# First attention: the row maxima from four 32-row tiles of TensorE, a head in each, and spread over the whole group

## The chip, the cores and the metric

The kernel runs on one core of one Trainium2 chip. The metric is the device time of one execution, in microseconds, read on that core. Three executions of the kernel before took 1702.1, 1706.09 and 1711.71 us; their median, 1706.09 us, is the time before.

## The reference

A two-layer transformer block on x of shape (4, 512, 256), with a context of the same shape and one mask row: an attention with 16 heads of 16, a mixture of 8 experts with top-1 routing, an attention with 16 heads of 64 and 128 memory rows, and three pairs of dequantized linear layers with LoRA. The change touches the first attention alone:

```python
qh = (q @ Wq.T + bq).reshape(Bq, Sq, H, Dh).transpose(0, 2, 1, 3)      # q = layernorm(x), H = 16, Dh = 16
kh = (k @ Wk.T + bk).reshape(Bq, Sk, H, Dh).transpose(0, 2, 1, 3)
attn = jnp.einsum('bhqd,bhkd->bhqk', qh, kh) * Dh ** -0.5
attn = jnp.where(causal_mask, -jnp.inf, attn)
attn = jax.nn.softmax(attn, axis=-1)
out = jnp.einsum('bhqk,bhkd->bhqd', attn, vh)
x = x + out.transpose(0, 2, 1, 3).reshape(Bq, Sq, D) @ Wo.T + bo
```

## The kernel before, in words

`attention0` goes through the batches (4) in a loop and in each through four groups of four heads. Everything is in one launch, with engines that meet at semaphores.

Queries and keys are projected half by half (8 heads) into `full`, and split into a high part `hi` (float32r) and a rest `lo` (L418). SyncE's DMAs then stack them by head into `q_stack` and `k_stack`, 128 partitions by head by 512: rows 0 to 15 hold hi and hi, rows 16 to 31 hi and lo, rows 48 to 63 lo and hi, the last row the negative row maximum of the queries against ones. One matmul over 128 rows (L602) so gives a head's scores less the row maximum for one key tile; a second (L604) adds the key mask. Six DMAs of 128 KB stack four heads' queries and keys (`stack`, L233, and `stack_last`, L241).

The softmax needs the row maximum first. For each head and each of the four query tiles one matmul (L579) over rows 0 to 126 writes 128 x 512 scores into one of the three banks of `p_m`, and VectorE adds the query mask and takes the maximum into `mx` (L424). After 16 of these, for the four heads of the group ahead, `mx` is transposed (L586), negated (L432) and brought into the last row of `q_stack` by a DMA (L248).

The order on TensorE is written out by hand in the table STEPS: eight parts per group, each with two score tiles of two heads. ScalarE takes the exponentials of a part (L334), TensorE multiplies them with the values in four column tiles of 32, one a head (`times_v`, L615), and for each group the row sums are spread (`sums`, L591), VectorE takes their reciprocal (L440) and multiplies (L442). `query` and `key` are the projections for the half ahead (in groups 0 and 2), `rows` the four transposes of the next batch's normalized x (in group 1), `turn` is L586. `maximum`, `turn`, `sums`, `rows`, `query` and `key` share the three banks in turn: an instruction that fills a bank waits until the reader of the fill three places before is done. VectorE's program goes through the same table.

After group 3 of a batch come its last `times_v` and `sums`, the values of the next batch (L569), and the output projection (L659), which waits for the last L442.

The functions that the diff touches, with the line numbers of the profile:

Of the kernel before, what the change touches and what calls it, by code (L numbers as in the profile page):

```python
# [5 lines left out]
F32 = mybir.dt.float32  # L6
# [9 lines left out]
P = 128  # L16
# [57 lines left out]
def attention0(nc, x_all, A, held):  # L74
# [9 lines left out]
    with ExitStack() as ctx:  # L84
# [6 lines left out]
        def sem(name):  # L91
# [43 lines left out]

        STEPS = (("query", "score", "score", "times_v", "maximum"),
                 ("key", "maximum", "score", "maximum", "score", "maximum"),
                 ("maximum", "score", "maximum", "score", "times_v", "maximum"),  # L140
                 ("maximum", "score", "maximum", "score", "maximum"),
                 ("maximum", "score", "maximum", "score", "times_v", "maximum"),
                 ("maximum", "score", "maximum", "score", "maximum"),
                 ("score", "score", "turn", "times_v"),
                 ("sums", "score", "score", "rows"))
        PARTS = len(STEPS)
        N_MAX = G0 * NT

        def steps(g, j, ahead):

            for what in STEPS[j]:
                if what in ("query", "key") and (g % 2 or g and not ahead):
                    continue

                if what == "rows" and (g != 1 or not ahead):
                    continue
                if what == "sums" and g == 0:
                    continue
                if what in ("maximum", "turn") and g + 1 >= NG0 and not ahead:
                    continue  # L160
                yield what

        FILLS = {"query": 1, "key": 1, "maximum": 1, "turn": 1, "rows": NT, "sums": 1}
        DVE_FILLS = {"maximum": 1, "rows": NT, "sums": 1}

        def fills(kinds, last_g=NG0 - 1):

            return sum(kinds.get(w, 0) for g in range(last_g + 1) for j in range(PARTS) for w in steps(g, j, True))


        BEFORE = NT + 2 + 2 + N_MAX + 1
        DVE_BEFORE = NT + 2 + N_MAX

        AT_END = 2 + 1 + NT // 2
        assert (fills(FILLS) + AT_END) % M_BANKS == 0
        x_in, weights_in, loaded = sem("x_in"), sem("weights_in"), sem("loaded")
        consts, prep = sem("consts"), sem("prep")
        zeroed, prefilled = sem("zeroed"), sem("prefilled")
# [6 lines left out]
        m_free = Count(sem("m_free"), fills(DVE_FILLS) + AT_END, DVE_BEFORE)  # L185
        hi_ready = Count(sem("hi_ready"), 4)
        split_ready = Count(sem("split_ready"), 4)
        stacked = [Count(sem("stacked_first"), 16 * 12), Count(sem("stacked_last"), 16 * 12)]
        mx_ready = Count(sem("mx_ready"), NG0)
        nm_ready = Count(sem("nm_ready"), NG0)  # L190
        nm_in = Count(sem("nm_in"), 16 * NG0)
# [17 lines left out]
        @block.sync  # L209
        def _(sp):  # L210
            def load_x(i):
                sp.dma_start(x_all[:, i * NT:(i + 1) * NT, :],
                             A["x"][i].rearrange("(t p) d -> p t d", p=P)).then_inc(x_in, 16)

            load_x(0)
            for dst, src in ((bqk[:], A["L0_bqk"]), (wq[:], A["L0_wq"]), (wk[:], A["L0_wk"])):
                sp.dma_start(dst, src).then_inc(weights_in, 16)
            sp.dma_start(ctx_t[:], A["ctx_t"][0]).then_inc(ctx_in.sem, 16)
            for dst, src in ((wv[:], A["L0_wv"]), (bv[:], A["L0_bv"].partition_broadcast(P)), (mask_in[:], A["mask"]),
                             (bo[:], A["L0_bo"].partition_broadcast(P)), (wo[:], A["L0_wo"])):  # L220
                sp.dma_start(dst, src).then_inc(loaded, 16)
            for i in range(1, B):
                load_x(i)

            halves = ((q_stack, (hi, hi, lo)), (k_stack, (hi, lo, hi)))

            def stack(b, half):

                at = 8 * (half % 2)
                for n, (stack, parts) in enumerate(halves):  # L230
                    split_ready.wait(sp, b, 2 * half + n + 1)
                    for k, part in enumerate(parts):
                        sp.dma_start(stack[DH0 * k:DH0 * (k + 1), at:at + G0, :].bitcast(F32),  # L233
                                     part[0:P // 2, n, :].bitcast(F32)).then_inc(stacked[0].sem, 16)

            def stack_last(half):

                at = 8 * (half % 2) + G0
                for n, (stack, parts) in enumerate(halves):
                    for k, part in enumerate(parts):  # L240
                        sp.dma_start(stack[DH0 * k:DH0 * (k + 1), at:at + G0, :].bitcast(F32),  # L241
                                     part[P // 2:P, n, :].bitcast(F32)).then_inc(stacked[1].sem, 16)

            def bring_maxima(b, g):

                nm_ready.wait(sp, b, g + 1)
                at = G0 * (g % NG0)
                sp.dma_start(q_stack[MAX_ROW:P, at:at + G0, :].bitcast(F32), neg_max[:].bitcast(F32))\  # L248
                  .then_inc(nm_in.sem, 16)

            def turn(b, ahead):
                for g in range(NG0):
                    if g % 2 == 0 and (ahead or g == 0):
                        stack(b, g // 2 + 1)
# [55 lines left out]
        def _(act):  # L310
# [6 lines left out]
            def project(b, half, n, m):  # L317


                split_ready.wait(act, b, 2 * half + n - 1)  # L320
                for count in stacked:
                    count.wait(act, b, 16 * 6 * half)
# [49 lines left out]
        def _(dve):  # L372
# [38 lines left out]
            def split(b, half, n):  # L411

                hi_ready.wait(dve, b, 2 * half + n + 1)

                if n == 0:
                    for count in stacked:
                        count.wait(dve, b, 16 * 6 * half)
                dve.tensor_tensor(lo[:, n, :], full[:, n, :], hi[:, n, :].bitcast(F32),  # L418
                                  ALU.subtract).then_inc(split_ready.sem, 1)

            def maximum(b, fill, i):
                m = fill.bank()
                m_full.wait_apart(dve, b, fill.n, prep, 5)
                dve.tensor_tensor_reduce(scratch[:, fill.n % M_BANKS, :], m, bias_q[:, i % NT, :], 1.0, -3.0e38, ALU.add,  # L424
                                         ALU.max, mx[:, i:i + 1]).then_inc(m_free.sem, 1)

            def turn_maxima(b, fill, g):
                m = fill.bank()
# [15 lines left out]
            def turn(b, ahead):  # L444
                fill = Fill()
                freed = 0
                for g in range(NG0):
                    i = 0
                    for j in range(PARTS):
                        for what in steps(g, j, ahead):  # L450
                            freed += DVE_FILLS.get(what, 0)
                            if what == "maximum":
                                maximum(b, fill, i)
                                i += 1
                            elif what == "turn":
                                turn_maxima(b, fill, g + 1)
                            elif what == "rows":
# [52 lines left out]
            for i in range(N_MAX):  # L510
                maximum(-1, fill, i)
            turn_maxima(-1, fill, NG0)
            dve.wait_ge(x_in, 16 * B)
            with dve.Fori(0, B - 1) as b:
                turn(b, True)
# [3 lines left out]
        def _(pe):  # L519
# [52 lines left out]

            def maximum(b, banks, g, i):

                h, t = G0 * (g % NG0) + i // NT, i % NT
                m = banks.free()
                if i == 0:
                    stacked[g % 2].wait(pe, b, 16 * 6 * (g // 2 + 1))
                done(pe.matmul(m, q_stack[0:MAX_ROW, h, P * t:P * (t + 1)], k_stack[0:MAX_ROW, h, :],  # L579
                               start=True, stop=True))  # L580

            def turn_maxima(b, banks, g):
                m = banks.free(nm_ready, g + 1)
# [35 lines left out]
            def turn(b, ahead):  # L619
# [2 lines left out]
                banks = Banks(b)  # L622
                banks.readers = [(m_free, -1), (m_free, 0), (m_free, 0)]
                for g in range(NG0):
                    i = 0
                    for j in range(PARTS):
                        head = 0
                        for what in steps(g, j, ahead):
                            if what in ("query", "key"):
                                project(b, banks, g // 2 + 1, ("query", "key").index(what))  # L630
                            elif what == "maximum":
                                maximum(b, banks, g + 1, i)
                                i += 1
                            elif what == "turn":
                                turn_maxima(b, banks, g + 1)
                            elif what == "score":
# [36 lines left out]
            for i in range(N_MAX):  # L673
                maximum(-1, banks, NG0, i)
            turn_maxima(-1, banks, NG0)
            with pe.Fori(0, B - 1) as b:
                turn(b, True)
            turn(B - 1, False)
# [1376 lines left out]
```

## Time and profile before

| | |
|---|---|
| time, three executions | 1702.1, 1706.09, 1711.71 us |
| the profiled execution's own time | 1709.27 us |
| its span, first to last instruction | 1707.6 us |
| mean granted TensorE clock | 0.929 |
| TensorE matmuls busy | 1480.1 us, 87% |
| TensorE weight loads busy | 881.2 us, 52% |
| VectorE busy | 904.5 us, 53% |
| ScalarE busy | 494.4 us, 29% |
| GpSimd busy | 451.0 us, 26% |
| first attention | about 0 to 437 us of the span |

The shares of the page are means over all stages, and the first attention is a quarter of the span. A matmul's record includes the time until its result has landed, so records of matmuls overlap: the pace at which TensorE works is read from the distance between starts. The idle time in brackets in a timeline is counted from the end of the record before, and so is shorter than the real hold-up. In a timeline neighbouring instructions of one line stand as one row with their count.

### The profile page before, as it was taken

Reading aid. Unit: us, or ns where it says so; the run is one execution under the profiler, and the core shown is the slowest. Engines: PE = TensorE matmul, PEld = TensorE weight load, DVE = VectorE, ACT = ScalarE, POOL = GpSimd, SP = SyncE. Lnnn points to the kernel's source line nnn. Section 1 sums busy time; section 2 is a strip of 40 time slices with the busy share of each in tenths; the row PEclk is TensorE's granted clock in tenths of the full one; section 3 lists DMA queues with packets and bytes.
Section 4 is the critical chain, followed back from the end, with each engine's and each line's share of the span. In section 5 each row is a group of like instructions: output and inputs, shape, how many; then the busy total and the mean of one; then the engine's idle time right before and its main releaser. Section 6 shows DMA issues by size and latency. Waiting matters only on the chain. (4 is left out here: it accounts for less than half of the span.)

```text
span 1707.6 us, 18955 instructions
## 1 busy us (share of the span) xinstructions
PE 1480.1 (87%) x6061; PEld 881.2 (52%) x6088; DVE 904.5 (53%) x1684; ACT 494.4 (29%) x618; POOL 451.0 (26%) x257
## 2 busy tenths in 40 slices
PE   5899898998719889874799999999999999976886
PEld 2334343443618777752444446444644465435775
DVE  5666666765420000015467664766576656736666
ACT  2443334444102222210133332333233323320221
POOL 2000000000240000022144442544344534552333
PEclk8999999999559999995799999999999999986998
DMA  6522113220374545335456555565356655302001
GB/s 157 140 38 37 32 19 50 37 38 1 130 247 144 180 155 182 135 64 90 81 74 87 74 79 69 76 86 69 43 74 86 82 67 68 44 0 102 1 0 50
DMA packets 62238, 136.14 MB, mean 80 GB/s; under 512 B 10593, under 2 KB 21217, under 8 KB 57569
## 3 DMA queue, kind: packets, MB, share of 16 engines
q1 hardware_dynamic: 59440, 127.26, 39.5%
q0 software_dynamic: 2736, 8.13, 1.4%
q8 instruction: 31, 0.51, 0.1%
q14 instruction: 31, 0.25, 0.1%
HBM read 58.55 MB, written 12.06 MB: 41 GB/s over the span
## 5 line engine op out<-in xcount | busy, mean ns | idle before, releaser
L1070 POOL TENSOR_TENSOR a_probs<-a_probs 128x1024 f32<-128x1024 f32 x128 | 304.2, 2376 | 415.6 <-PE a_p_os L1633 415.1
L1141 ACT ACTIVATE a_probs<-a_p_s 128x1024 f32<-128x1024 f32 x160 | 163.7, 1023 | 378.9 <-PE a_p_s L1619 378.9
L1352 DVE TENSOR_REDUCE a_max_ctx<-a_p_m 128x1 f32<-128x512 f32 x256 | 169.9, 688 | 79.8 <-PE a_p_m L1594 76.7
L424 DVE CUSTOM_DVE_ANT_0 a_scratch<-a_p_m,a_bias_q 128x512 bf16<-128x512 f32 x256 | 163.1, 687 | 80.6 <-PE a_p_m L579 80.5
L334 ACT ACTIVATE a_probs<-a_p_s 128x1024 f32<-128x1024 f32 x128 | 130.5, 1024 | 140.8 <-PE a_p_s L604 135.9
L579 PE MATMUL a_p_m<-a_k_stack,a_q_stack 127*128 127x512 f32 x256 | 128.0, 543 | 14.5 <-DVE a_mx L424 7.0
L1633 PE MATMUL a_p_os<-a_probs,a_v 128*64 128x512 f32 x512 | 138.1, 618 | 0.0
L1514 PE MATMUL a_p_s<-a_o_raw,a_w 128*128 128x256 f32 x480 | 123.8, 392 | 13.8 <-DVE a_o_raw L1283 13.8
L1594 PE MATMUL a_p_m<-a_k_hl,a_q_hh 128*128 128x512 f32 x256 | 111.0, 481 | 18.6 <-DVE a_v L1330 8.2
L1288 DVE TENSOR_TENSOR a_yb<-a_p_os,a_yb 128x512 f32<-128x512 f32 x15 | 10.4, 692 | 218.9 <-PE a_p_os L1523 218.9
L1523 PE MATMUL a_p_os<-a_w,a_probs 128*128 128x256 f32 x480 | 118.6, 380 | 0.6 <-ACT a_probs L1118 0.6
L1618 PE MATMUL a_p_s<-a_q_hh,a_k_hl 128*128 128x512 f32 x256 | 118.5, 463 | 0.0
L602 PE MATMUL a_p_s<-a_q_stack,a_k_stack 128*128 128x512 f32 x256 | 117.4, 487 | 1.0 <-DMA a_q_stack<-a_neg_max 0.9
L1375 DVE RECIPROCAL a_recip<-a_p_os 128x512 f32<-128x512 f32 x32 | 106.8, 3336 | 16.6 <-PE a_p_os L1643 16.6
L1514 PEld LDWEIGHTS a_p_s<-a_o_raw,a_w 128*128 128x128 f32 x480 | 92.6, 195 | 30.2 <-DVE a_o_raw L1283 17.6
L1594 PEld LDWEIGHTS a_p_m<-a_k_hl,a_q_hh 128*128 128x128 f32 x256 | 46.6, 195 | 109.0 <-DVE a_max_ctx L1352 53.1
L1619 PE MATMUL a_p_s<-a_q_lm,a_k_h 65*128 65x512 f32 x256 | 102.2, 399 | 0.0
L1118 ACT ACTIVATE a_probs<-a_p_s,a_b 128x256 f32<-128x256 f32 x120 | 55.9, 473 | 151.0 <-PE a_p_s L1514 150.9
L1523 PEld LDWEIGHTS a_p_os<-a_w,a_probs 128*128 128x128 f32 x480 | 91.2, 190 | 14.1 <-ACT a_probs L1118 1.8
L604 PE MATMUL a_p_s<-a_bias_k,a_ident_b 128*128 128x512 bf16 x229 | 90.0, 393 | 0.0
L579 PEld LDWEIGHTS a_p_m<-a_k_stack,a_q_stack 127*128 127x128 f32 x256 | 47.2, 198 | 66.5 <-DVE a_mx L424 45.7
L1343 DVE SCALAR_TENSOR_TENSOR a_lo<-a_p_m,a_bqk,a_hi 128x512 fp32r<-128x512 f32 x58 | 43.0, 747 | 59.0 <-ACT a_hi L1131 54.2
(200 smaller groups left out, 2162.0 us busy)
## 6 DMA issues: line engine op xcount, KB each, us to landing
a_w<-in_L_w SPq DMA_DIRECT2D x30, 1024.0 KB, 8.0
a_q_hh<-a_hi SPq DMA_DIRECT2D x64, 256.0 KB, 5.6
a_k_hl<-a_hi SPq DMA_DIRECT2D x32, 256.0 KB, 8.0
a_k_hl<-a_lo SPq DMA_DIRECT2D x32, 256.0 KB, 9.5
a_k_h<-a_hi SPq DMA_DIRECT2D x32, 256.0 KB, 10.6
a_q_lm<-a_lo SPq DMA_DIRECT2D x32, 256.0 KB, 7.1
a_ctx_t<-in_ctx_t SPq DMA_DIRECT2D x8, 512.0 KB, 5.7
a_q_stack<-a_hi SPq DMA_DIRECT2D x32, 128.0 KB, 3.9
```

The source lines that it names most:

```text
L334: act.activation(probs[:, j % 4, :, :], p_s[:, j % 2, :, :], ACT.Exp).then_inc(exp_done.sem, 1)
L424: dve.tensor_tensor_reduce(scratch[:, fill.n % M_BANKS, :], m, bias_q[:, i % NT, :], 1.0, -3.0e38, ALU.add, ALU.max, mx[:, i:i + 1]).then_ ...
L579: done(pe.matmul(m, q_stack[0:MAX_ROW, h, P * t:P * (t + 1)], k_stack[0:MAX_ROW, h, :], start=True, stop=True))
L602: pe.matmul(p_s[:, slot, i, :], k_stack[:, h, P * kt:P * (kt + 1)], q_stack[:, h, :], start=True, stop=False)
L1070: pool.tensor_tensor(probs[:, kt], probs[:, kt - 1], probs[:, kt], ALU.add)\
L1141: act.activation(probs[:, kt, :, :], p_s[:, (KT1 * p + kt) % 2, :, :], ACT.Exp).then_inc(exp_done.sem, 1)
L1352: dve.tensor_reduce(max_ctx[:, NT * head + t:NT * head + t + 1], m, AX, ALU.max)\
L1514: mm = pe.matmul(p_h[:, c % 4, 0:CT], w1[:, r, k, P * c:P * (c + 1)], rows_t[:, r % 2, k, :], start=(k == 0), stop=(k == DC - 1))
L1523: mm = pe.matmul(p_y[:, t, 0:D], hidden[:, d % 4, P * t:P * (t + 1)], w2[:, r, d, :], start=(d == 0), stop=(d == FC - 1))
L1594: done(pe.matmul(m, q_hh[:, s, P * t:P * (t + 1)], k_hl[:, s, :], start=True, stop=True))
L1618: pe.matmul(p_s[:, n % 2, i, :], first, q_hh[:, s, :], start=True, stop=False)
L1633: mm = pe.matmul(p_o[DK * i:DK * (i + 1), :], vh, probs[:, kt, i, :], start=(kt == 0), stop=(kt == KT1 - 1))
```

## The change: what it does

The maxima are taken from the high parts alone. The high parts of a group's four heads now lie in four different 32-row strips of the stacks (rows 0 to 15, 32 to 47, 64 to 79, 96 to 111), so that a maximum's matmul reads 16 rows of its head's strip and runs in a 32-row tile of the array; successive maxima go through the four heads. For this the DMAs that stack a half's queries and keys are cut differently: four of 32 KB and two of 128 KB in place of three of 128 KB. The table spreads the maxima in runs of three and two after the scores; the first two of a group's sixteen (`early`) are taken in the last part of the group before, where `sums` now stands behind the scores and behind these two.

```diff
-        STEPS = (("query", "score", "score", "times_v", "maximum"),
-                 ("key", "maximum", "score", "maximum", "score", "maximum"),
...
-                 ("sums", "score", "score", "rows"))
+        STEPS = (("query", "score", "score", "times_v", "maximum", "maximum", "maximum"),
+                 ("key", "score", "score", "maximum", "maximum", "maximum"),
...
+                 ("score", "score", "early", "early", "sums", "rows"))
+        EARLY = sum(step.count("early") for step in STEPS)
...
-            halves = ((q_stack, (hi, hi, lo)), (k_stack, (hi, lo, hi)))
+            def fill(n, at, rows, landed):
+
+                stack, parts = ((q_stack, (hi, lo)), (k_stack, (lo, hi)))[n]
+                for i in range(G0):
+                    sp.dma_start(stack[32 * i:32 * i + DH0, at + i, :].bitcast(F32),
+                                 hi[rows + i:rows + P // 2:G0, n, :].bitcast(F32)).then_inc(landed, 16)
+                for k, part in zip((1, 3), parts):
+                    sp.dma_start(stack[DH0 * k:DH0 * (k + 1), at:at + G0, :].bitcast(F32),
+                                 part[rows:rows + P // 2, n, :].bitcast(F32)).then_inc(landed, 16)
...
             def maximum(b, banks, g, i):
 
-                h, t = G0 * (g % NG0) + i // NT, i % NT
+                tile, t = i % G0, i // G0
+                h, rows = G0 * (g % NG0) + tile, slice(32 * tile, 32 * tile + DH0)
                 m = banks.free()
                 if i == 0:
-                    stacked[g % 2].wait(pe, b, 16 * 6 * (g // 2 + 1))
-                done(pe.matmul(m, q_stack[0:MAX_ROW, h, P * t:P * (t + 1)], k_stack[0:MAX_ROW, h, :],
-                               start=True, stop=True))
+                    stacked[g % 2].wait(pe, b, LANDED * (g // 2 + 1))
+                done(pe.matmul(m, q_stack[rows, h, P * t:P * (t + 1)], k_stack[rows, h, :], start=True, stop=True))
```

TensorE where group 2 of a batch ends and group 3 begins, before. L591 spreads the sums of the group before, L602 and L604 are the scores and their mask, L615 is `times_v`, L579 a maximum:

```order
L591 MATMUL a_p_m<-a_o_norm,a_spread 128x512
L602 MATMUL a_p_s<-a_q_stack,a_k_stack 128x512
L604 MATMUL a_p_s<-a_bias_k,a_ident_b 128x512
...
L615 MATMUL a_p_o<-a_probs,a_v 32x512 x4
L63 REGISTER_ALU
L579 MATMUL a_p_m<-a_k_stack,a_q_stack 128x512 x2
L602 MATMUL a_p_s<-a_q_stack,a_k_stack 128x512
L604 MATMUL a_p_s<-a_bias_k,a_ident_b 128x512
L63 REGISTER_ALU
L579 MATMUL a_p_m<-a_k_stack,a_q_stack 128x512
```

The same place with the change; L603 is now the sums, L614 and L616 the scores, L627 `times_v`, L592 a maximum:

```order
L614 MATMUL a_p_s<-a_q_stack,a_k_stack 128x512
L616 MATMUL a_p_s<-a_bias_k,a_ident_b 128x512
L63 REGISTER_ALU x2
L592 MATMUL a_p_m<-a_k_stack,a_q_stack 128x512 x2
L603 MATMUL a_p_m<-a_o_norm,a_spread 128x512
L63 REGISTER_ALU x2
L614 MATMUL a_p_s<-a_q_stack,a_k_stack 128x512
...
L627 MATMUL a_p_o<-a_probs,a_v 32x512 x4
L63 REGISTER_ALU
L592 MATMUL a_p_m<-a_k_stack,a_q_stack 128x512
...
L592 MATMUL a_p_m<-a_k_stack,a_q_stack 128x512
L63 REGISTER_ALU
L592 MATMUL a_p_m<-a_k_stack,a_q_stack 128x512
```

Two maxima now stand ahead of the sums, and the sums stand behind the part's scores instead of ahead of them. Between the sums and the third maximum after them lie one part's scores and `times_v`, where there were two parts' scores, `times_v` and more.

SyncE's queue for one half of a batch, before (the first four heads, the maxima of the group ahead, the last four heads):

```order
L233 DMA a_q_stack<-a_hi 16x4x512 x2
L233 DMA a_q_stack<-a_lo 16x4x512
L63 REGISTER_ALU
L233 DMA a_k_stack<-a_hi 16x4x512
L233 DMA a_k_stack<-a_lo 16x4x512
L233 DMA a_k_stack<-a_hi 16x4x512
L63 REGISTER_ALU
L248 DMA a_q_stack<-a_neg_max 1x16x128
```

And with the change:

```order
L233 DMA a_q_stack<-a_hi 16x512 x4
L236 DMA a_q_stack<-a_hi 16x4x512
L236 DMA a_q_stack<-a_lo 16x4x512
L63 REGISTER_ALU
L233 DMA a_k_stack<-a_hi 16x512 x4
L236 DMA a_k_stack<-a_lo 16x4x512
L236 DMA a_k_stack<-a_hi 16x4x512
L63 REGISTER_ALU
L254 DMA a_q_stack<-a_neg_max 1x16x128
```

Twelve DMAs are issued for four heads instead of six.

## Rows read from the trace of the kernel before

**Rows 1.** Busy time by stretch: PE, PEld, DVE, ACT, POOL, then granted clock
```profile
44.00:437.00 393.00, 354.57 (x1531) 164.40 (x1557) 253.07 (x612) 156.82 (x172) 10.18 (x6) 0.96 0.23 42
```

**Rows 2.** Groups by line, 44 to 437 us: busy, mean ns, idle before
```profile
L579 PE MATMUL a_p_m<-a_k_stack,a_q_stack 127*128 127x512 f32 x240 | 118.3, 527 | 8.1 <-DVE a_mx L424 7.0
```

**Rows 3.** TensorE's timeline around one `times_v`: start, length, instructions
```profile
50.68 0.39 PE L602 MATMUL a_p_s<-a_q_stack,a_k_stack 128*128 128x512 f32 x1
50.91 0.39 PE L604 MATMUL a_p_s<-a_bias_k,a_ident_b 128*128 128x512 bf16 x1
51.23 1.07 PE L615 MATMUL a_p_o<-a_probs,a_v 128*32 128x512 f32 x8
52.23 0.72 PE L579 MATMUL a_p_m<-a_k_stack,a_q_stack 127*128 127x512 f32 x2
52.79 0.39 PE L602 MATMUL a_p_s<-a_q_stack,a_k_stack 128*128 128x512 f32 x1
```

**Rows 4.** The same timeline: a key projection, four passes of 512 columns
```profile
94.04 1.88 PE L560 MATMUL a_p_m<-a_ctx_t,a_wk 128*128 128x512 f32 x4
```

**Rows 5.** A matmul in a 32-row tile, and what follows it
```profile
L1915 PE MATMUL f_p_y<-f_lora_b,f_lora_a x24: 629/629/791, 1550.6 to 1568.0; 32*128 32x256 f32 x24
1568.58 1.57 PEld L1934 LDWEIGHTS f_p_t<-f_ident,f_h 128*128 128x128 f32 x8 [0.65 <-issue]
```

**Rows 6.** Timeline, start of group 3: TensorE, then VectorE
```profile
109.88 1.13 PE L591 MATMUL a_p_m<-a_o_norm,a_spread 128*128 128x512 f32 x2
...
113.05 1.06 PE L615 MATMUL a_p_o<-a_probs,a_v 128*32 128x512 f32 x8 [0.19 <-ACT a_probs L334]
114.04 0.74 PE L579 MATMUL a_p_m<-a_k_stack,a_q_stack 127*128 127x512 f32 x2
...
111.04 3.36 DVE L440 RECIPROCAL a_recip<-a_p_m 128x512 f32<-128x512 f32 x1 [1.68 <-PE a_p_m L591]
114.44 0.69 DVE L442 TENSOR_TENSOR a_o_norm<-a_o_norm,a_recip 128x512 f32<-128x512 f32 x1
115.05 0.68 DVE L424 CUSTOM_DVE_ANT_0 a_scratch<-a_p_m,a_bias_q 128x512 bf16<-128x512 f32 x1
...
115.66 0.68 DVE L424 CUSTOM_DVE_ANT_0 a_scratch<-a_p_m,a_bias_q 128x512 bf16<-128x512 f32 x1
```

**Rows 7.** Timeline of TensorE, end of group 1: sums, third row transpose
```profile
80.40 1.13 PE L591 MATMUL a_p_m<-a_o_norm,a_spread 128*128 128x512 f32 x2
...
84.98 0.44 PE L546 MATMUL a_p_m<-a_ident,a_xn 128*128 128x128 f32 x2 [2.08 <-DVE a_recip L440]
```

**Rows 8.** Timeline, end of a batch
```profile
128.03 1.13 PE L591 MATMUL a_p_m<-a_o_norm,a_spread 128*128 128x512 f32 x2
...
131.19 1.06 PE L615 MATMUL a_p_o<-a_probs,a_v 128*32 128x512 f32 x8 [1.11 <-ACT a_probs L334]
...
138.43 0.89 PE L659 MATMUL a_p_m<-a_wo,a_o_norm 128*128 128x256 f32 x3 [0.81 <-DVE a_o_norm L442]
...
134.20 3.36 DVE L440 RECIPROCAL a_recip<-a_p_m 128x512 f32<-128x512 f32 x1 [0.92 <-PE a_p_m L591]
```

**Rows 9.** Timeline of TensorE: the transpose of the maxima
```profile
126.82 0.28 PE L586 MATMUL a_p_m<-a_ident,a_mx 128*16 128x128 f32 x1 [0.19 <-DVE a_mx L424]
```

**Rows 10.** DMA issues in group 2, and their median time to landing
```profile
99.41 1.18 SPq L233 DMA_DIRECT2D a_q_stack<-a_hi  x2
...
103.45 0.60 SPq L233 DMA_DIRECT2D a_k_stack<-a_hi  x1
...
a_k_stack<-a_hi SPq DMA_DIRECT2D x2, 128.0 KB, 4.3
```

**Rows 11.** Timeline of TensorE: the longest wait of a maximum for a bank
```profile
73.37 0.50 PE L579 MATMUL a_p_m<-a_k_stack,a_q_stack 127*128 127x512 f32 x1 [1.18 <-DVE a_mx L424]
```

**Rows 12.** Before the loop: a stacking DMA and the first maximum
```profile
23.50 0.60 SPq L233 DMA_DIRECT2D a_k_stack<-a_hi  x1
...
29.49 9.83 PE L579 MATMUL a_p_m<-a_k_stack,a_q_stack 127*128 127x512 f32 x16 [6.34 <-DMA a_k_stack<-a_hi]
```

More of the change, by code:

```diff
@@ L132, in attention0 @@
         p_o = ps("p_o", [P, S])
-        STEPS = (("query", "score", "score", "times_v", "maximum"),
-                 ("key", "maximum", "score", "maximum", "score", "maximum"),
[L140 to L143, printed above, removed]
+        STEPS = (("query", "score", "score", "times_v", "maximum", "maximum", "maximum"),
+                 ("key", "score", "score", "maximum", "maximum", "maximum"),
+                 ("score", "score", "maximum", "maximum", "times_v"),
+                 ("score", "score", "maximum", "maximum"),
+                 ("score", "score", "maximum", "maximum", "times_v"),
+                 ("score", "score", "maximum", "maximum"),
                  ("score", "score", "turn", "times_v"),
-                 ("sums", "score", "score", "rows"))
+                 ("score", "score", "early", "early", "sums", "rows"))
+        EARLY = sum(step.count("early") for step in STEPS)
         PARTS = len(STEPS)
@@ L160, in steps @@
                     continue
+                if what == "early" and g + 2 >= NG0 and not ahead:
+                    continue
                 yield what
-        FILLS = {"query": 1, "key": 1, "maximum": 1, "turn": 1, "rows": NT, "sums": 1}
-        DVE_FILLS = {"maximum": 1, "rows": NT, "sums": 1}
+        FILLS = {"query": 1, "key": 1, "maximum": 1, "early": 1, "turn": 1, "rows": NT, "sums": 1}
+        DVE_FILLS = {"maximum": 1, "early": 1, "rows": NT, "sums": 1}
         def fills(kinds, last_g=NG0 - 1):
             return sum(kinds.get(w, 0) for g in range(last_g + 1) for j in range(PARTS) for w in steps(g, j, True))
-        BEFORE = NT + 2 + 2 + N_MAX + 1
-        DVE_BEFORE = NT + 2 + N_MAX
+        BEFORE = NT + 2 + 2 + N_MAX + 1 + EARLY
+        DVE_BEFORE = NT + 2 + N_MAX + EARLY
         AT_END = 2 + 1 + NT // 2
         assert (fills(FILLS) + AT_END) % M_BANKS == 0
+        LANDED = 16 * 2 * (G0 + 2)
         x_in, weights_in, loaded = sem("x_in"), sem("weights_in"), sem("loaded")
@@ L187, in attention0 @@
         split_ready = Count(sem("split_ready"), 4)
-        stacked = [Count(sem("stacked_first"), 16 * 12), Count(sem("stacked_last"), 16 * 12)]
+        stacked = [Count(sem("stacked_first"), 2 * LANDED), Count(sem("stacked_last"), 2 * LANDED)]
         mx_ready = Count(sem("mx_ready"), NG0)
@@ L223, in _ @@
                 load_x(i)
-            halves = ((q_stack, (hi, hi, lo)), (k_stack, (hi, lo, hi)))
+            def fill(n, at, rows, landed):
[6 more added lines that the diff above has]
+                                 part[rows:rows + P // 2, n, :].bitcast(F32)).then_inc(landed, 16)
             def stack(b, half):
-                at = 8 * (half % 2)
-                for n, (stack, parts) in enumerate(halves):
+                for n in range(2):
                     split_ready.wait(sp, b, 2 * half + n + 1)
-                    for k, part in enumerate(parts):
-                        sp.dma_start(stack[DH0 * k:DH0 * (k + 1), at:at + G0, :].bitcast(F32),
-                                     part[0:P // 2, n, :].bitcast(F32)).then_inc(stacked[0].sem, 16)
+                    fill(n, 8 * (half % 2), 0, stacked[0].sem)
             def stack_last(half):
[L238 to L242, printed above, removed]
+                for n in range(2):
+                    fill(n, 8 * (half % 2) + G0, P // 2, stacked[1].sem)
             def bring_maxima(b, g):
@@ L321, in project @@
                 for count in stacked:
-                    count.wait(act, b, 16 * 6 * half)
+                    count.wait(act, b, LANDED * half)
                 at = half % 2
@@ L416, in split @@
                     for count in stacked:
-                        count.wait(dve, b, 16 * 6 * half)
+                        count.wait(dve, b, LANDED * half)
                 dve.tensor_tensor(lo[:, n, :], full[:, n, :], hi[:, n, :].bitcast(F32),
@@ L423, in maximum @@
                 m_full.wait_apart(dve, b, fill.n, prep, 5)
-                dve.tensor_tensor_reduce(scratch[:, fill.n % M_BANKS, :], m, bias_q[:, i % NT, :], 1.0, -3.0e38, ALU.add,
-                                         ALU.max, mx[:, i:i + 1]).then_inc(m_free.sem, 1)
+                h, t = i % G0, i // G0
+                dve.tensor_tensor_reduce(scratch[:, fill.n % M_BANKS, :], m, bias_q[:, t, :], 1.0, -3.0e38, ALU.add,
+                                         ALU.max, mx[:, NT * h + t:NT * h + t + 1]).then_inc(m_free.sem, 1)
             def turn_maxima(b, fill, g):
@@ L447, in turn @@
                 for g in range(NG0):
-                    i = 0
+                    i, early = EARLY, 0
                     for j in range(PARTS):
@@ L454, in turn @@
                                 i += 1
+                            elif what == "early":
+                                maximum(b, fill, early)
+                                early += 1
                             elif what == "turn":
@@ L512, in _ @@
             turn_maxima(-1, fill, NG0)
+            for i in range(EARLY):
+                maximum(-1, fill, i)
             dve.wait_ge(x_in, 16 * B)
@@ L624, in turn @@
                 for g in range(NG0):
-                    i = 0
+                    i, early = EARLY, 0
                     for j in range(PARTS):
@@ L633, in turn @@
                                 i += 1
+                            elif what == "early":
+                                maximum(b, banks, g + 2, early)
+                                early += 1
                             elif what == "turn":
@@ L675, in _ @@
             turn_maxima(-1, banks, NG0)
+            for i in range(EARLY):
+                maximum(-1, banks, NG0 + 1, i)
             with pe.Fori(0, B - 1) as b:
```

## The prediction

> **What bounds the kernel now.** I read the busy time by stretch first. In the first attention, the only place that changes, TensorE is busy 355 of 393 us at a granted clock of 0.96, VectorE 253, ScalarE 157 [rows 1]. So TensorE's program sets the time, and everything behind the attention starts when it ends. The groups by line then say what a maximum is there: 240 matmuls in the loop, that is 15 groups of 16, with little idle time of TensorE directly before them [rows 2]. The record of one is 527 ns, but that is latency. The pace is in the timeline: L602 and L604 start 0.23 us apart [rows 3]. Sixteen maxima cost 3.7 us of a group of some 18 us.
>
> **The burst in a 32-row tile, and its price.** The change lets two or three maxima of different heads stream at once: in the best case a run of two or three costs one stream, 0.21 us, in place of 0.46 or 0.69. The same trace shows what another tile shape between full-array matmuls costs, with the column tiles of `times_v`. L604 starts at 50.91 and needs 0.23; the next full-array matmul starts at 52.23, 1.09 us later; the two streams in it are 2 x 0.43 = 0.86, as (1.88 - 0.16) / 4 = 0.43 for one pass of 512 columns [rows 4], 0.16 being a record's tail (0.39 - 0.23). Behind it two maxima take 0.56 instead of 0.46 [rows 3]. So two changes of tile shape cost 0.23 + 0.10 = 0.33 us: the queue that otherwise loads weights under the running matmul stands until the array is empty, and the first load is then uncovered. Row tiles are seen once: the last matmul of L1915 starts at 1568.0 and streams some 0.43 us, at the lower clock level; the next load, in full shape, comes at 1568.58, 0.15 us after, and the weight queue's idle time of 0.65 is put to no other engine [rows 5]. A gap there as well.
>
> A run between full-array matmuls thus costs 0.21 + 0.33, and 0.10 more since its own weights have 128 columns where those of `times_v` have 32: 0.64. Against 0.46 for two that is +0.18, against 0.69 for three -0.05. A run beside a `times_v` adds one change of shape only, some 0.44: -0.02 for two, -0.25 for three. A group has three lone pairs, one lone triple, two pairs and one triple beside `times_v`: 3 x 0.18 - 0.05 - 0.04 - 0.25 = +0.2 us. For 15 groups **+3.0 us**: the overlap is eaten by the changes of shape.
>
> The Trainium skill (TensorEngine Tiling (Array Packing), Key Properties) says that a change of tiling mode drains TensorE while tiles of one mode run independently. No run here shows it for a pair of row tiles; the column tiles agree, with 0.33 us for two changes. It makes a free change of shape, the fast rival below, the less likely.
>
> **The sums behind the scores.** Three banks go round, and the third maximum after the sums waits for VectorE's reciprocal.
> - Group 3, which has no projection to fill the time. From the start of the sums the reciprocal ends 4.56 us later (109.88 to 114.44) [rows 6]. TensorE has then done sums 0.86, two score tiles 4 x 0.23 = 0.93, `times_v` 0.95 with its change of shape and another 0.2: it is at the first maximum after 3.0 and at the third at once, and waits 1.55. VectorE starts on them at 5.17 (115.05) and needs 0.61 each (115.05 to 115.66) [rows 6], as before, so of the later holding up I add 0.2. The wait of `times_v` for ScalarE, 0.25 with the start of L604 and the bracket of 0.19 [rows 6], goes, as the two early maxima and the sums now lie between. 1.5 us in each of three batches (the last has no maxima there): **+4.4**.
> - Group 1, with the row transposes. The third transpose starts 4.58 us after the sums do (80.40 to 84.98), held 2.08 us by the reciprocal's bank [rows 7]. The scores that were under this wait now stand ahead of the sums: 0.93 each in three batches, **+2.8**.
> - The end of a batch. Scores, early pair, sums and `times_v` now follow each other, where `times_v` waited (bracket 1.11) [rows 8]. But VectorE gets the sums late: its first reciprocal starts 0.93 + 0.5 + 1.16 = 2.6 us into the part, is done with the product at 2.6 + 4.0 = 6.6 to 6.8, and the second, which starts at 134.20 - 128.03 = 6.17 now [rows 8], moves by 0.6, and L659 with it. The early pair, counted at 0.64 above, is inside that. **0**.
>
> **The transpose of the maxima.** It waits for the last maximum (bracket 0.19, about 0.35 by the starts) [rows 9]. The last pair arrives together, so VectorE needs 2 x 0.61 after it, while TensorE has two score tiles: 0.1 more for each of 15 groups, **+1.5**.
>
> **Stacking.** SyncE needs about 0.6 to 0.64 us for each issue (1.18 for two) [rows 10]. In groups 0 and 2 the first `early` needs the stack of that same half. Before, the first issue is at 99.41, the last at 103.45, landed 4.3 later, ahead of the group's end at 109.88. Now VectorE reaches the split two maxima later (1.2 us), and the last issue stands 11 x 0.64 = 7.0 behind the first: 99.41 + 1.2 + 7.0 + 4.3 = 111.9. TensorE is there at 109.88 + 0.93 + 0.3 = 111.1. With the semaphore's way I take 0.9, seven times: **+6.3**. The ends are 0 (DMAs of 32 KB that land sooner) and 2.4 each, if landing takes the 6.0 us of the start, 23.50 to 29.49 [rows 12].
>
> **Before the loop.** The first maximum waits for the stack [rows 12]. Six more issues stand ahead, 3.8 us; landing takes 4.3 instead of 6.0 if the engines are less behind, so between +2.1 and +3.8. I take 2.8, and 0.5 for the two early maxima there: **+3.3**.
>
> **Waits for a bank inside a group.** With three maxima a part VectorE needs 1.83 us where a part without `times_v` gives 1.6; the longest wait is 1.5 us (bracket 1.18) [rows 11]. With two it needs 1.22 and these waits go, but the first two parts now hold three each in one run, which only VectorE's pace of 0.61 serves. I set these against each other: **0**, ends -7 and +3 over all.
>
> The sum is 3.0 + 4.4 + 2.8 + 1.5 + 6.3 + 3.3 = **+21 us**: 1709.3 (span 1707.6 and 1.7 around it) + 21 = 1731 for the profiled execution, which lies 3.2 over the median; from the median 1706.1 it is 1728.
>
> **Rivals.**
> - *Changes of shape are free for row tiles (the other side).* Then a run costs 0.21 and no more, 11 changes of shape a group go from the sum, 11 x 0.165 x 15 = 27 us, of which I leave 3 to the banks, as TensorE then comes sooner to the same reciprocal. 1728 - 24 = 1704, no slower than before; with the stacks in time 1698. It decides from a price below about 0.05 us a change. For it: the array's rows are separate tiles with weights of their own. Against: 0.33 at every `times_v` [rows 3], and the gap at 1568.58 [rows 5].
> - *Row tiles don't overlap.* Nine more streams a group, 9 x 0.21 x 15 = 28 us, of which a third lies in waits for VectorE: +19, 1747. Against: the column tiles do overlap, eight matmuls in 1.07 us [rows 3].
> - *The stack lands late*, at its upper end, 7 x 1.5 = +10: 1738.
> - *Nothing runs in a row tile*: 16 x 0.23 a group as before, less 3 us of the sum, 1725; little apart from the forecast, and in its chance.
>
> The Trainium skill (TensorE: Matmul & The Clock Gate, Part 3) reports four row tiles of K = 32 at 3.07 times the speed of one after another. By that a run of two or three costs hardly more than one stream, which is the value in the sum; no run here shows it.
>
> **How the numbers follow.** Forecast 0.50 (1728, its own range 1716 to 1738), free changes 0.24 (1698 to 1707), no overlap 0.14, late stack 0.12. The range 1703 to 1748 leaves out the fastest of the free cases and the worst of the slow ones. A change of 0.5% is 8.5 us, about what can be told from none: faster 0.11 and same 0.15, nearly all from the second case and the low edge of the forecast; slower 0.74.
>
> **What would show it.** Right: in the new timeline the matmul after a run of two starts about 0.85 us after the L604-like one before the run; the third maximum of group 3 stands 1.5 us for the reciprocal; `early` in groups 0 and 2 waits for a DMA; the batch takes some 6 us more than now; times behind the attention are unchanged. Wrong: weight loads of a run start under the scores before it, runs of 0.2 us, and a group shorter than now.

## The result, and the profile after

The changed kernel takes 1767.3 us (median of 4, 1764.5 to 1769.9) against 1708.9 us for the kernel before on the same chip: a ratio of 1.0347, 95% interval 1.0309 to 1.0386. It is slower by 3.5%. The forecast was slower by 21 us, range 1703 to 1748. The sign is right, the size is not, and the time lies outside the range. One of the twelve executions of e5 below took 4924 us and is left out of its numbers.

Behind the attention nothing moved. The stretch from the end of the last output projection (L659) to the end of the span, in the kernel before:

```profile
439.00:1708.00 1269.00, 1100.38 (x4472) 703.14 (x4472) 627.96 (x1011) 326.78 (x440) 429.06 (x236) 0.92 0.46 89
```

and of the changed kernel, with its attention (answering to [rows 1]) and two of its groups. The columns are length, busy time of PE, PEld, DVE, ACT and POOL, granted clock, DMA share, GB/s:

```profile
44.00:499.00 455.00, 400.28 (x1538) 164.12 (x1565) 254.10 (x612) 155.78 (x172) 10.20 (x6) 0.88 0.13 37
499.00:1769.00 1270.00, 1099.27 (x4472) 701.57 (x4472) 628.47 (x1011) 326.75 (x440) 428.85 (x236) 0.92 0.46 89
302.00:321.00 19.00, 17.34 (x80) 6.22 (x81) 13.61 (x45) 8.41 (x10) 3.39 (x2) 1.00 0.34 81
351.00:378.00 27.00, 24.09 (x83) 8.27 (x83) 14.71 (x36) 8.77 (x10) 0.00 (x0) 0.75 0.16 39
```

All of it is in the attention, which from 44 us on takes 455 us where it took 395 (44 to 439), and the granted clock there is 0.88 where it was 0.96. A group is counted here from one transpose of the maxima to the next. One that keeps the clock (302 to 321) takes 19.2 us, where the same group of before took 18.5; one that loses it (351 to 378) takes 26.8, where it took 18.1. The granted clock is a mix of the two levels 2.4 and 1.2 GHz. (1 - clock) x length is the most that the lower level can have cost, as if TensorE had never waited there: 55 us now, 16 before.

The timeline of TensorE shows the mechanics at full clock, first a lone pair and the transpose, answering to [rows 3, 9], then the start of a group 3, to [rows 6]:

```profile
318.82 0.39 PE L616 MATMUL a_p_s<-a_bias_k,a_ident_b 128*128 128x512 bf16 x1
319.14 0.50 PE L592 MATMUL a_p_m<-a_k_stack,a_q_stack 16*128 16x512 f32 x2
319.58 0.50 PE L614 MATMUL a_p_s<-a_q_stack,a_k_stack 128*128 128x512 f32 x1
319.92 0.39 PE L616 MATMUL a_p_s<-a_bias_k,a_ident_b 128*128 128x512 bf16 x1
...
321.15 0.28 PE L598 MATMUL a_p_m<-a_ident,a_mx 128*16 128x128 f32 x1 [0.38 <-DVE a_mx L431]
...
354.46 0.50 PE L592 MATMUL a_p_m<-a_k_stack,a_q_stack 16*128 16x512 f32 x2 [0.59 <-DMA a_k_stack<-a_hi]
354.88 1.12 PE L603 MATMUL a_p_m<-a_o_norm,a_spread 128*128 128x512 f32 x2
...
359.74 0.50 PE L592 MATMUL a_p_m<-a_k_stack,a_q_stack 16*128 16x512 f32 x1 [1.37 <-DVE a_recip L447]
...
361.29 1.80 PE L592 MATMUL a_p_m<-a_k_stack,a_q_stack 16*128 16x512 f32 x3
363.02 0.80 PE L614 MATMUL a_p_s<-a_q_stack,a_k_stack 128*128 128x512 f32 x1
363.61 0.65 PE L616 MATMUL a_p_s<-a_bias_k,a_ident_b 128*128 128x512 bf16 x1
```

The pair's record is 0.50 us for two, where a lone one takes 0.50 too (359.74): they stream together. From L616 to the score behind the pair it is 0.76, of which 0.23 are L616 itself, and the next distance is 0.34 instead of 0.23: 0.64 us for the pair. The early pair waits for a stacking DMA. The third maximum behind the sums waits for the reciprocal and starts 4.86 us after them. Then comes something that no term had: after three maxima at VectorE's pace (361.29) the same L616 takes a record of 0.65 instead of 0.39. The array runs at half clock from here.

The same course in the first batch, windows of the changed kernel (the early pair there waits 0.89 for its DMA):

```profile
68.92 0.50 PE L592 MATMUL a_p_m<-a_k_stack,a_q_stack 16*128 16x512 f32 x2 [0.89 <-DMA a_k_stack<-a_hi]
...
70.00:74.00 4.00, 3.44 (x19) 1.11 (x17) 3.83 (x16) 2.40 (x3) 1.02 (x1) 1.00 0.44 103
74.00:81.00 7.00, 6.77 (x19) 2.17 (x19) 5.07 (x18) 1.20 (x2) 0.00 (x0) 0.55 0.46 117
```

### The profile page after: what moved, and what is told of

Read it like the earlier page. It is cut to its first block and busy times, and to the rows that moved or that the text cites. A ratio compares the mean times of both kernels' runs of the same rounds, so it can differ in the third digit from the quotient of the medians.

```text
span 1768.3 us, 19048 instructions
## 1 busy us (share of the span) xinstructions
PE 1521.2 (86%) x6061; PEld 877.0 (50%) x6088; DVE 905.8 (51%) x1684; ACT 493.4 (28%) x618; POOL 450.9 (25%) x257
## 5 line engine op out<-in xcount | busy, mean ns | idle before, releaser
L614 PE MATMUL a_p_s<-a_q_stack,a_k_stack 128*128 128x512 f32 x256 | 143.6, 621 | 0.0
L592 PE MATMUL a_p_m<-a_k_stack,a_q_stack 16*128 16x512 f32 x256 | 82.6, 563 | 23.4 <-DMA a_k_stack<-a_hi 12.0
L616 PE MATMUL a_p_s<-a_bias_k,a_ident_b 128*128 128x512 bf16 x229 | 96.8, 423 | 0.0
L614 PEld LDWEIGHTS a_p_s<-a_q_stack,a_k_stack 128*128 128x128 f32 x256 | 55.0, 215 | 71.3 <-issue 36.7
L627 PE MATMUL a_p_o<-a_probs,a_v 128*32 128x512 f32 x512 | 77.4, 680 | 0.8 <-ACT a_probs L340 0.8
```

The costliest lines, as they stand in the source:

```text
L614: pe.matmul(p_s[:, slot, i, :], k_stack[:, h, P * kt:P * (kt + 1)], q_stack[:, h, :], start=True, stop=False)
```

## The experiments

Times are medians; the ratio is to the kernel before, run beside it, which stood at 1708.1 to 1710.2. "Clock" is the granted clock in the profile from 44 us to the end of the attention's last output projection, "lost" is (1 - clock) x length there, an upper bound, known to about 2 us by the rounding. "Whole" is the granted clock of a whole execution, the median of all of them; 0.001 of it is 1.7 us.

| kernel | us | ratio, 95% interval | clock | lost, us | whole |
|---|---|---|---|---|---|
| before | 1709 | | 0.96 | 16 | 0.929 |
| changed | 1767.3 | 1.0347 (1.0309 to 1.0386) | 0.88 | 55 | 0.910 |
| e1 order only | 1720.5 | 1.0072 (1.0052 to 1.0091) | 0.96 | 16 | 0.928 |
| e2 full tiles | 1728.5 | 1.0109 (1.0090 to 1.0129) | 0.96 | 17 | 0.929 |
| e3 32 rows | 1759.5 | 1.0297 (1.0278 to 1.0315) | 0.91 | 40 | 0.915 |
| e4 sums first | 1739.5 | 1.0184 (1.0159 to 1.0208) | 0.94 | 25 | 0.922 |
| e5 order, sums first | 1713.0 | 1.0021 (1.0009 to 1.0032) | 0.96 | 16 | 0.929 |
| e6 same tile | 1770.4 | 1.0350 (1.0327 to 1.0373) | 0.89 | 50 | 0.912 |
| e7 rows, old order | 1749.2 | 1.0231 (1.0214 to 1.0247) | 0.94 | 26 | 0.924 |
| e8 filler | 1766.9 | 1.0325 (1.0306 to 1.0343) | 0.93 | 32 | 0.920 |
| e9 even table | 1698.5 | 0.9941 (0.9922 to 0.9960) | 0.98 | 8 | 0.933 |
| e10 66 rows | 1739.3 | 1.0167 (1.0140 to 1.0193) | 0.92 | 34 | 0.924 |
| e11 64 rows | 1753.8 | 1.0244 (1.0212 to 1.0275) | 0.93 | 31 | 0.923 |
| e12 DMAs only | 1710.1 | 1.0005 (0.9990 to 1.0019) | 0.96 | 16 | 0.929 |

An interval reaches 2 to 5 us to either side (7 for the changed kernel), so a difference of a few us between two rows of the table is rough.

The theory after the result: the clock falls because matmuls over 16 rows do not keep it up (A). The rival: it falls because TensorE stands in more and longer waits, whatever its matmuls are (B).

**e1, the order without the row tiles.** The stacks are those of before, three DMAs of 128 KB for queries and three for keys:

```diff
-                stack, parts = ((q_stack, (hi, lo)), (k_stack, (lo, hi)))[n]
...
+                stack, parts = ((q_stack, (hi, hi, lo)), (k_stack, (hi, lo, hi)))[n]
...
-                done(pe.matmul(m, q_stack[rows, h, P * t:P * (t + 1)], k_stack[rows, h, :], start=True, stop=True))
+                done(pe.matmul(m, q_stack[0:MAX_ROW, h, P * t:P * (t + 1)], k_stack[0:MAX_ROW, h, :], start=True, stop=True))
```

> The new order with the two early maxima, but the maxima as before: full-array matmuls over 127 rows of the old stacks, six DMAs of 128 KB for four heads. Theory A (the clock falls because matmuls of 16 rows in row tiles do not keep it up): the granted clock in the first attention is back at about 0.95 or more, and what is left over the kernel before are the waits of the order, by the prediction's terms 4 to 10 us: 1713 to 1719. Theory B (the clock falls because TensorE now stands in more and longer waits, whatever the tile): clock near 0.88 there and 1735 or more. The DMA wait of the first early maximum is gone or under 0.3 us, since six issues end 3.8 us sooner.

Measured 1720.5, clock 0.96. The clock is back, as A expected, and the order by itself costs 12 us, a little over A's 1713 to 1719.

**e2, full-array maxima in the changed kernel.** Only the last two lines of e1's diff.

> The changed kernel with one edit: each maximum is a full-array matmul over 127 rows of the new stacks; order, DMAs and waits are those of the changed kernel. Theory A: clock in the first attention at 0.94 or more; the time is that of the new order alone and of the later stacks, 1718 to 1728, 40 to 50 us under the changed kernel. Theory B: the clock stays near 0.88, and the time is 1755 or more, as only the changes of tile shape go and the overlap with them.

Measured 1728.5, at the upper end of what A expected, 39 us under the changed kernel. The long waits are still there. The timeline of e2 in the first batch has them, the early pair's even longer than the 0.89 of the changed kernel:

```profile
66.42 0.72 PE L592 MATMUL a_p_m<-a_k_stack,a_q_stack 127*128 127x512 f32 x2 [1.37 <-DMA a_k_stack<-a_hi]
...
71.17 1.72 PE L592 MATMUL a_p_m<-a_k_stack,a_q_stack 127*128 127x512 f32 x3 [0.28 <-DVE a_mx L431]
72.73 0.39 PE L614 MATMUL a_p_s<-a_q_stack,a_k_stack 128*128 128x512 f32 x1
```

and the windows of e2 over the stretches shown of the changed kernel keep the full clock (the same work stands about 3 us earlier in e2):

```profile
70.00:74.00 4.00, 3.49 (x13) 1.58 (x12) 3.93 (x15) 1.17 (x2) 1.02 (x1) 1.00 0.52 115
74.00:81.00 7.00, 7.00 (x39) 2.96 (x37) 5.62 (x19) 3.50 (x4) 2.41 (x1) 1.00 0.17 59
```

B in its plain form falls: waits of this length do not bring the clock down when the maxima use 127 rows.

**e3, 32 rows of the strip.**

```diff
-                h, rows = G0 * (g % NG0) + tile, slice(32 * tile, 32 * tile + DH0)
+                h, rows = G0 * (g % NG0) + tile, slice(32 * tile, 32 * tile + 32)
```

> The changed kernel with maxima over 32 rows of a head's strip instead of 16; the same tile, the same order. The upper rows hold the rest parts for two heads and zeros against ones for the two others. If the clock follows how many rows of the array work (a form of theory A), it falls less and the time is 5 to 20 us under 1767. If it follows only that the matmuls stand in row tiles and overlap, or only the waits (theory B), the time is 1767 within 4.

Measured 1759.5: 8 us under the changed kernel, with a clock of 0.91. More rows, less loss. The places of the falls vary from batch to batch of the loop, but the clock of the whole execution says the same in all four: 0.914 to 0.916, against 0.910 in all four of the changed kernel.

**e4, the sums ahead of the scores again, row tiles kept.**

```diff
-                 ("score", "score", "early", "early", "sums", "rows"))
+                 ("sums", "score", "score", "early", "early", "rows"))
```

> The changed kernel with the sums ahead of the last part's scores again, the early maxima behind them. By the prediction the third maximum of group 3 waits 1.5 us less and the row transposes 0.9 us less a batch: 5 to 8 us under 1767 at an equal clock. Theory B: with these waits gone the clock falls less too, and it is 15 us or more under. Theory A: the clock in group 3 stays near 0.7, and the gain is 5 to 8 us.

Measured 1739.5, 28 us less, clock 0.94. This is B's number. Waits do matter for the clock where the maxima use 16 rows: with the maxima's wait for the reciprocal gone, the loss falls from 55 to 25 us. Neither theory holds alone.

**e5, the same edit in e1**, so with full-array maxima and the old stacks.

> The new order with full-array maxima and the old stacks (as e1_order_only, 1720.5), and the sums ahead of the last part's scores again. The prediction's term of the sums behind the scores (4.4 + 2.8 us) goes: 1712 to 1715, level with the kernel before or up to 0.5% slower. If the sums' place costs only through the clock, which stood at 0.96 in e1, nothing changes: 1720.

Measured 1713.0: 7.5 us less than e1, at the same clock (8.7 by the ratios). That is the bare price of the sums' place, against 7.2 in the prediction (4.4 + 2.8). It leaves about 20 us of e4 for the clock.

**e6, the runs in one tile.**

```diff
-                h, t = i % G0, i // G0
+                h, t = i // NT, i % NT
...
-                tile, t = i % G0, i // G0
+                tile, t = i // NT, i % NT
```

The first pair of lines is VectorE's program, the second TensorE's.

> The changed kernel, but the maxima go through the query tiles of one head before the next head, so that two or three in a run are in the same 32-row tile and stream one after another; 16 rows each, as in the changed kernel. Theory A1 (what keeps the clock up is the time in which the array streams anything): nine more streams of 0.21 us a group cost up to 28 us at an equal clock, but the half-clock time shrinks from about 75 us to 40 or less: 1750 to 1772. Theory A2 (what counts is how much of the array works, so that 16 rows count little whether they overlap or not): as much half-clock time as in the changed kernel or more, 1780 to 1800. If row tiles did not overlap in the first place, the time is 1767 and the half-clock time unchanged.

Measured 1770.4, the upper end of A1's range and under A2's, with 50 us lost to the clock instead of 55; A1 wanted at most 20 (40 us at half clock). In its timeline a pair, 0.50 in the changed kernel, takes 0.73:

```profile
321.23 0.73 PE L592 MATMUL a_p_m<-a_k_stack,a_q_stack 16*128 16x512 f32 x2
```

So the overlap in the changed kernel is real and saves about 0.23 us a pair, and longer streaming of 16 rows helps the clock little if at all: 0.912 against 0.910 over the whole execution. Neither form fits: A1 has the loss wrong, A2 the time.

**e7, row tiles in the old table.** `STEPS` of before, `early` gone with it.

> The kernel before with the row tiles alone: the new stacks and maxima of 16 rows in row tiles, heads in turn, but the table of before, where most maxima stand alone between two scores. Each lone maximum changes the array's shape twice: 0.64 - 0.23 = 0.41 us more, some 11 lone runs a group, less the waits for banks that this fills: 35 to 70 us over before at an equal clock (1743 to 1778), and more where the clock falls.

Measured 1749.2, 40 us over before, clock 0.94: inside the range, at its low end, although some of it is the clock (26 lost against 16).

**e8, more work.**

```diff
+                if lead:
+                    pe.matmul(m, q_stack[0:MAX_ROW, h, P * t:P * (t + 1)], k_stack[0:MAX_ROW, h, :],
+                              start=True, stop=True)
                 done(pe.matmul(m, q_stack[rows, h, P * t:P * (t + 1)], k_stack[rows, h, :], start=True, stop=True))
```

`lead` is set for the first maximum of each run in the loop.

> The changed kernel with more work: in the loop, the first maximum of each run is preceded by a full-array matmul of 127 rows into the same bank, which the maximum then overwrites (its result is not used). Seven more streams of 0.23 us a group are 24 us at an equal clock. If the clock falls for want of array work in the runs, the half-clock time drops from about 75 us to 35 or less and gives most of it back: 1750 to 1770. If it falls for another reason the time is 1785 to 1795 and the half-clock time stays.

Measured 1766.9, level with the changed kernel although 105 full-array matmuls are added to the loop; the clock rises from 0.88 to 0.93, the loss falls from 55 to 32 us. The 24 us expected of the added work are about what the clock gives back.

**e10 and e11, 66 and 64 rows.** The shape splits between them: 66 rows are a full-array matmul, 64 rows a 64-row tile.

```diff
-                done(pe.matmul(m, q_stack[rows, h, P * t:P * (t + 1)], k_stack[rows, h, :], start=True, stop=True))
+                done(pe.matmul(m, q_stack[0:66, h, P * t:P * (t + 1)], k_stack[0:66, h, :], start=True, stop=True))
```

> The changed kernel with maxima over rows 0 to 65 of the stacks in the full-array shape (not every head's high parts are in these, so the maxima are not those of the reference). Order, DMAs and waits as in e2_full_tiles. If the clock falls with the rows in use, half-clock time between e2's 38 us and the changed kernel's 110, and 1735 to 1750. If it falls only with a small tile shape, as e2: 1728 within 3.

> As e10_rows66 with rows 0 to 63, which is a 64-row tile: two rows fewer, another shape, with changes of shape around each run. The tiles of a run do not overlap, all being the same. At an equal clock that is e2's time and the changes of shape, about 1738. If the rows in use set the clock, half-clock time as in e10; if the shape does, near the changed kernel's, and 1755 to 1770.

e10 measured 1739.3, 11 us over e2 (10 by the ratios), which has the same shape, order and DMAs and differs by the rows alone; 34 us are lost to the clock instead of 17. TensorE's waits in the attention are alike in both: 7.1 and 7.0 us in all for the stacking DMA, 4.4 and 4.4 in front of maxima for the reciprocal. With the shape held, the rows move the clock; whether it is their number or the data in them was not tried apart. e11 has the same clock (0.924 and 0.923 over the whole execution) and is another 14 us slower, which is the price of its changes of shape (10 were expected). So the rows move the clock and the shape sets the changes; each costs by itself.

In e10 a fall is seen right behind the early pair's wait of 1.52, where e2 waited 1.37 and kept the clock; the timeline of e10:

```profile
68.69 0.73 PE L592 MATMUL a_p_m<-a_k_stack,a_q_stack 66*128 66x512 f32 x2 [1.52 <-DMA a_k_stack<-a_hi]
...
69.97 0.39 PE L616 MATMUL a_p_s<-a_bias_k,a_ident_b 128*128 128x512 bf16 x1
70.29 1.75 PE L627 MATMUL a_p_o<-a_probs,a_v 128*32 128x512 f32 x8
```

`times_v` takes 1.75 with the fall in it, where it takes 1.07 at full clock.

**e12, the new DMAs alone.** The table of before, full-array maxima, the new stacks.

> The kernel before with the new stacks alone: twelve DMAs for four heads, full-array maxima over 127 rows, the table of before without early maxima. e2 less e1 put the twelve DMAs at 8 us in the new order, where the first early maximum waits for them. If that wait is their whole cost, only the 2 us before the loop stay: 1710 to 1712. If they cost by themselves (SyncE's queue holding up the maxima's DMA, traffic against the engines), 1715 or more.

Measured 1710.1 against 1710.2 (0.9990 to 1.0019). Twelve DMAs instead of six cost nothing that can be told from the noise in the old order. In the new one they cost e2 less e1, 8.0 us; TensorE's seven waits of the early maxima for them add up to 7.0 us in e2, and e1 has no such wait.

**e9, another table for the kernel before.** No early maxima, two in the short parts and four where `times_v` stands:

```diff
-        STEPS = (("query", "score", "score", "times_v", "maximum"),
-                 ("key", "maximum", "score", "maximum", "score", "maximum"),
-                 ("maximum", "score", "maximum", "score", "times_v", "maximum"),
-                 ("maximum", "score", "maximum", "score", "maximum"),
...
+        STEPS = (("query", "score", "score", "times_v", "maximum", "maximum"),
+                 ("key", "score", "maximum", "score", "maximum"),
+                 ("maximum", "score", "maximum", "score", "maximum", "times_v", "maximum"),
+                 ("score", "maximum", "score", "maximum"),
...
```

> The kernel before with another table and nothing else: full-array maxima, old stacks, sums first, no early maxima, sixteen maxima spread 2, 2, 4, 2, 4, 2 over the first six parts, four where times_v stands and two where it does not. VectorE needs 2.44 and 1.22 us for them, TensorE's parts last about 3.0 and 1.4, so the waits of the kernel before for a bank inside a group (1.5 us in group 1, 0.8 in group 2, 0.6 in group 0) should go: 3 us a batch, 1697 to 1702. If VectorE's backlog behind the reciprocal just moves the wait, 1706 to 1709.

Measured 1698.5, faster than both kernels: 0.9941 (0.9922 to 0.9960). The window of its attention, answering to [rows 1]:

```profile
44.00:428.00 384.00, 352.81 (x1538) 161.95 (x1564) 255.41 (x613) 156.23 (x172) 10.18 (x6) 0.98 0.22 43
```

and its maxima in the groups by line, answering to [rows 2]:

```profile
L579 PE MATMUL a_p_m<-a_k_stack,a_q_stack 127*128 127x512 f32 x240 | 123.1, 535 | 3.5 <-DVE a_mx L424 2.1
```

The idle time for the banks falls from 7.0 to 2.1 us in TensorE's records, that of the transposes of the maxima from 3.2 to 0.4, and the clock rises to 0.98. The loss by the clock falls by at most 8 of the 11 us. The shorter waits have a part of their own: at full clock a group takes 17.9 us from transpose to transpose (61.26 to 79.11), where the same group takes 18.5 before (60.66 to 79.20). Why the even table holds the clock better was not tried apart from it.

## Why the prediction was wrong

The parts of the 58 us, by differences of medians. The last row is the one that went wrong:

| step | predicted | measured | from |
|---|---|---|---|
| order and early maxima, without row tiles and DMAs | 4.4 + 2.8 + 1.5 + 0.5 = 9.2 | 12 | e1 less before |
| of it, the sums behind the scores | 7.2 | 7.5 | e1 less e5 |
| twelve DMAs, in the group and before the loop | 6.3 + 2.8 = 9.1 | 8.0 | e2 less e1 |
| row tiles instead of full-array maxima | 3.0 | 39 | changed less e2 |

- **Changes of shape.** Right: 0.64 us for a lone pair was forecast and is in the trace; the overlap is eaten by the changes of shape. In a group that keeps the full clock the whole term can be read: 19.21 us from transpose to transpose in the changed kernel (301.94 to 321.15), 19.01 in e2, +0.2 as forecast. It is one group. The row of e2:

```profile
279.13 0.28 PE L598 MATMUL a_p_m<-a_ident,a_mx 128*16 128x128 f32 x1 [0.36 <-DVE a_mx L431]
...
298.14 0.28 PE L598 MATMUL a_p_m<-a_ident,a_mx 128*16 128x128 f32 x1 [0.36 <-DVE a_mx L431]
```

The rivals "free changes" and "no overlap" are both out, by that row and by e6.
- **The sums.** The waits are right: the third maximum stands 4.86 us after the sums, and against the kernel before a group 3 of e1 is 1.6 us longer (19.7 and 18.1 from transpose to transpose), where 1.5 + 0.1 were forecast. That e1 less e5 comes to 7.5 us is partly luck. A group 3 is only 0.4 us shorter in e5, where a wait for a bank stands in the place of the one for the reciprocal, and the ends of the batches, which the prediction put at 0, give some 3.5 us, about half of it a fall of the clock that e1 has in its second batch and e5 has not.
- **The transpose.** Right in kind: the bracket rose from 0.19 to 0.38. The 15 brackets add up to 3.2 us before and 5.6 in e1, so +2.4 where 1.5 were forecast.
- **Stacking.** Right for the group (brackets 0.59 to 0.89 and the 8.0 us). What it costs before the loop (2.8 forecast) stays open: in the profiles the first transpose comes at 42.57 us in e12 and at 40.45 before, but the medians of e12 show no loss, with an interval from -1.7 to +3.2 us.
- **The rest of e1.** e5 is 4.0 us over before, where the terms left in it make 1.5 + 0.5. The 2 us over them are within the noise. The waits for a bank inside a group were set to 0 with ends of -7 and +3. From transpose to transpose the group 3 of e5 is 1.2 us longer than before and the group of 60 to 79 us is 0.7 shorter, so they cancel in part. In the timeline of e5, in a group 3, a maximum behind the sums waits for VectorE, bracket 0.84:

```profile
115.30 0.50 PE L589 MATMUL a_p_m<-a_k_stack,a_q_stack 127*128 127x512 f32 x1
116.63 1.11 PE L589 MATMUL a_p_m<-a_k_stack,a_q_stack 127*128 127x512 f32 x2 [0.84 <-DVE a_mx L428]
```

- **The step that failed** is the price of the burst: 0.21 + 0.33 + 0.10 us and the whole sum were worked out from rows of a kernel with a granted clock of 0.96, and no term, bound or rival asked whether the clock would stay there. It fell to 0.88. The last row of the table measured 39 us where 3 were forecast. The loss by the clock makes up to 55 - 17 = 38 of them in the two profiles, and up to 36 by the clocks of the whole executions (0.910 of 1766 us against 0.929 of 1727 us), which leaves 1 to 3 for the tiles themselves. Without the clock's part the changed kernel stands some 20 us over before, and 21 is what the prediction added up: its sum is about right for the old clock, and the clock is what it left out.

What brings the clock down is shown as two conditions that go together: maxima over few rows (e2 against the changed kernel; e10 against e2 with shape and order the same) and waits beside them (e4). By what rule the chip joins the two was not tried.

## What to carry to other kernels

Before TensorE's work is made cheaper or smaller, ask what it does to the clock: at the lower level the eight matmuls of `times_v` took 1.94 us (at 78.40 in the changed kernel) instead of 1.07, and here the clock was up to two thirds of the loss (38 of 58 us). By the prices measured here small tiles pay only where many of them stand together, since each change of shape cost about 0.2 us and the overlap of a pair saved 0.23; no run here has such a place. Where a matmul feeds a slower engine through few buffers, spread the matmuls by that engine's pace; a table alone gave 0.6% (e9).

## What the runs showed of the hardware

- Matmuls of 512 columns over 66 rows hold the clock up worse than over 127 rows, with the same shape, length and place: 0.92 against 0.96 in the attention, 11 us. Over 16 rows, in 32-row tiles, it is 0.88.
- Two matmuls in different 32-row tiles, each into its own bank, stream together: the pair's record is 0.50 us, and 0.73 when both are in one tile.
- Around row tiles the two changes of shape cost 0.43 us (0.64 for a run less its one stream of 0.21), against the 0.33 around the column tiles of [rows 3]. The prediction put the difference down to wider weights; no run tried that apart.
- Adding 105 full-array matmuls to the loop of the changed kernel left its time unchanged (1766.9 against 1767.3), while the granted clock rose by 0.05.
